# A selective-scan block on one core: the rows of each state's sum divided between ScalarE and VectorE block by block

## What is computed

```python
xz = hidden @ in_proj_w.T;  x, z = split(xz)          # 512 + 512 channels
u = silu(conv1d(x) + b)                               # causal, 4 taps
dt_low, B, C = split(u @ x_proj_w.T)                  # 16, 16, 16
delta = softplus(dt_low @ dt_proj_w.T + dt_b)
h = exp(delta * A) * h + delta * B * u                # per token, 512 channels x 16 states
y = sum over the 16 states of h * C  +  u * D
out = (y * silu(z)) @ out_proj_w.T
x1 = layernorm(hidden + out)                          # then router, experts, second layernorm
```

## Time and profile before

| | us |
|---|---|
| three runs | 4684.85, 4686.34, 4697.28 (median 4686.34) |
| the profiled execution, whole | 4683.41 |
| its span, first to last instruction | 4681.5 |
| eight chunks in the middle of stage 1 | 866.87 |
| busy in the whole span: PE, DVE, ACT, POOL | 3739.5, 3996.9, 3393.0, 3574.0 |

### The profile page before, as it was taken

The page is one execution under the profiler, slowest core; times in us unless marked ns, Lnnn a source line. Parts: engine busy times, 40 slices in busy tenths (PEclk is TensorE's granted clock), DMA queues, the critical chain, the costliest instruction groups (busy, mean ns, idle before and its releaser), DMA issues. The chain is left out here.

```text
span 4681.5 us, 57838 instructions
## 1 busy us (share of the span) xinstructions
PE 3739.5 (80%) x19154; PEld 2596.0 (55%) x19154; DVE 3996.9 (85%) x5099; ACT 3393.0 (72%) x5732; POOL 3574.0 (76%) x1744
## 2 busy tenths in 40 slices
PE   7888888888888888888888878888863199999990
PEld 3455555555555555555555555555553178888880
DVE  4999999999999999999999999999994667766645
ACT  5888787888888888878887888888861056555555
POOL 3888888888888888888888888888881156666643
PEclk8889898989888988988898998989875599999995
DMA  2454555554445545545554445545442123333328
GB/s 69 118 127 126 127 125 132 126 127 126 117 122 138 133 120 133 126 117 127 134 130 125 121 119 133 137 122 136 124 112 48 50 46 64 70 60 62 63 33 291
DMA packets 166374, 528.78 MB, mean 113 GB/s; under 512 B 31920, under 2 KB 97584, under 8 KB 118720
## 3 DMA queue, kind: packets, MB, share of 16 engines
q0 software_dynamic: 56832, 268.99, 29.5%
q1 hardware_dynamic: 104640, 239.32, 14.8%
q10 hardware_dynamic: 4608, 16.78, 0.9%
HBM read 221.47 MB, written 68.68 MB: 62 GB/s over the span
## 5 line engine op out<-in xcount | busy, mean ns | idle before, releaser
L369 POOL TENSOR_TENSOR dbu<-du,bb 128x2048 f32<-128x2048 f32 x512 | 2361.8, 4634 | 298.8 <-DVE h L736 274.0
L736 DVE TENSOR_TENSOR_SCAN h<-da,hlast,dbu 128x512 f32<-128x512 f32 x1536 | 1881.4, 1267 | 53.0 <-POOL dbu L369 41.9
L656 PE MATMUL ht<-ident,h 128*128 128x128 f32 x8192 | 1320.7, 308 | 594.6 <-DVE h L736 347.2
L419 ACT ACTIVATE da<-dl,negA 128x512 f32<-128x512 f32 x2048 | 1418.7, 698 | 468.9 <-DVE h L736 463.3
L656 PEld LDWEIGHTS ht<-ident,h 128*128 128x128 f32 x8192 | 1042.5, 157 | 1075.9 <-DVE h L736 555.2
L744 DVE SCALAR_TENSOR_TENSOR pair<-ht,ct,pair 128x512 f32<-128x512 f32 x896 | 639.0, 731 | 85.8 <-PE ht L656 85.4
L736 DVE TENSOR_TENSOR_SCAN h<-da,dbu 128x512 f32<-128x512 f32 x512 | 596.1, 1205 | 39.8 <-ACT da L419 25.0
L442 ACT ACTIVATE pair<-ht,ct 128x512 f32<-128x512 f32 x896 | 591.8, 687 | 50.7 <-PE ht L656 48.4
L589 PE MATMUL spare<-xin,win 128*128 128x512 f32 x1024 | 499.2, 617 | 40.3 <-DMA xin<-in_xt 26.0
L595 PE MATMUL spare<-xh,conv 128*128 128x512 f32 x1024 | 460.8, 592 | 2.2 <-ACT dl L456 1.5
L1149 POOL DMA_INDIRECT sums<-ot,idx x128 | 237.2, 1853 | 172.3 <-DVE ot L1425 130.7
(11 more groups left out here) (162 smaller groups left out, 5688.3 us busy)
## 6 DMA issues: line engine op xcount, KB each, us to landing
acc<-pair POOLq DMA_DIRECT2D x224, 1024.0 KB, 7.1
bb<-b_rows SPq DMA_DIRECT2D x128, 1024.0 KB, 5.2
xin<-in_xt SPq DMA_DIRECT2D x32, 512.0 KB, 4.4
xres<-in_x SPq DMA_DIRECT2D x32, 512.0 KB, 4.1
x_scores<-xres SPq DMA_DIRECT2D x32, 512.0 KB, 5.4
sums<-xres SPq DMA_DIRECT2D x32, 512.0 KB, 7.1
wraw<-in_w SPq DMA_DIRECT2D x16, 1024.0 KB
rows<-sums SPq DMA_DIRECT2D x32, 512.0 KB, 6.3
```

What stands on the lines that cost most here:

```text
L369: pool.tensor_tensor(dbu[n % 2][:], du[q][:], bb[part % 2][:, m:m + 1, :].to_broadcast([P, DT, CH]), ALU.mult).then_inc(dbu_done, 1)
L419: act.activation(da[DA_SLOT[m]][:], dl[q][:, dt, :], ACT.Exp, scale=negA[:, dt, n:n + 1]).then_inc(exp_done, 1)
L656: last = te.transpose(ht[HT_SLOT[m]][:, dt * P:(dt + 1) * P], h[n % 2][:, dt, b * P:(b + 1) * P], ident[:])
L736: dve.tensor_tensor_scan(h[n % 2][:, dt, :], da[DA_SLOT[n * DT + dt]][:], dbu[n % 2][:, dt, :], start, ALU.mult, ALU.add).then_inc(scan_do ...
```

## The change

The unit of division is no longer the state but the row block (n, b). Two new tables say which blocks ScalarE scales and VectorE adds, and in which slot: `SCALE_AT` has 36 blocks to a chunk (nine states' worth), `MAC_AT` 28 (seven). For each b by itself a block that is scaled starts a new sum and the added ones behind it belong to it, so each block row has nine sums (`TILE`), and a chunk has eight transfers that add, not seven. The sums have three homes besides `acc` of the chunk itself (`HOME`): `pair0`, `pair1` and the `acc` of the other parity, which is free between the turning of chunk c-1 and the start of chunk c+1. `add_sum` waits for both engines' last block of the sum, and the slots of the additions (`ADD_AT`) are new; slot 16 + n is slot n of the chunk behind. An adding block waits only for the scaled block that started its own row (`started_by`), where it used to wait for the same b of the state before.

The tables `STEPS`, `ACT_AT`, `DVE_AT` and `POOL_AT` are dealt anew, `BETWEEN` says how many of TensorE's steps in a slot come ahead of the fourth block's turning, and `xin` gets a second buffer, so that it is loaded a chunk earlier. No other instruction is added or removed.

```diff
-KIND = "ADADADADADADADAD"
-SUMS = KIND.count("A")
-ADD_AT = {t: min(LAST_OF[t] + 3, 17) for t in range(1, SUMS)}
+SCALE_AT = {(0, 0): [(14, 1)], (0, 2): [(15, 1), (15, 2)], (0, 3): [(15, 3)], (1, 2): [(0, 0), (0, 1)],
...
+MAC_AT = {(0, 1): [(15, 0)], (2, 1): [(1, 0), (1, 1)], (2, 2): [(1, 2)], (2, 3): [(1, 3)], (3, 3): [(2, 2)],
...
+ADD_AT = {1: 6, 2: 7, 3: 10, 4: 12, 5: 14, 6: 15, 7: 17, 8: 19}
+BETWEEN = [0, 1, 2, 2, 0, 1, 2, 0, 0, 0, 0, 2, 1, 2, 1, 1]
+TILE = {(n, b): sum((m, b) in ACT_ORDER for m in range(n + 1)) - 1 for n in range(16) for b in range(NB)}
+TILES = tile_of(15, 0) + 1
+HOME = [2, 0, 1, 3, 0, 1, 3, 0, 1, 0][:TILES]
+def started_by(n, b):
+
+    return next(k for k, (m, x) in enumerate(ACT_ORDER) if x == b and tile_of(m, x) == tile_of(n, b)) + 1
...
-        xin = a.sb("xin", [P, 2, CH])
+        xin = [a.sb(f"xin{i}", [P, 2, CH]) for i in range(2)]
...
+        def sum_tile(q, t):
+
+            return pair[HOME[t]] if HOME[t] < 2 else acc[q] if HOME[t] == 2 else acc[1 - q]
...
-                    pool.wait_ge(s, v)
-                    if not (is_first(c) and t == 1):
-                        pool.wait_ge(acc_in, 16 * (c * (SUMS - 1) + t - 1))
+                    pool.wait_ge(mac_done, c * N_DVE + macs_before_add(t))
+                    if scales_before_add(t):
+                        pool.sem_inc(pool_passed, 1)
+                        pool.wait_ge(scaled, c * N_ACT + scales_before_add(t))
+                    if not (is_first(c) and t == 1):
+                        pool.sem_inc(pool_passed, 1)
+                        pool.wait_ge(acc_in, 16 * (c * (TILES - 1) + t - 1))
...
-                    dve.wait_ge(scaled, c * N_ACT + scaled_by(n, b))
+                    dve.wait_ge(scaled, c * N_ACT + started_by(n, b))
```

More of the change, by code:

```diff
@@ new lines, with in_order @@
+MAC_AT = {(0, 1): [(15, 0)], (2, 1): [(1, 0), (1, 1)], (2, 2): [(1, 2)], (2, 3): [(1, 3)], (3, 3): [(2, 2)],
[4 rows of a table added]
+ADD_AT = {1: 6, 2: 7, 3: 10, 4: 12, 5: 14, 6: 15, 7: 17, 8: 19}
+BETWEEN = [0, 1, 2, 2, 0, 1, 2, 0, 0, 0, 0, 2, 1, 2, 1, 1]
+def in_order(table):
+    here = [(n, b) for slot in sorted(table) for n, b in table[slot] if n < slot[0]]
+    return here + [(n, b) for slot in sorted(table) for n, b in table[slot] if n >= slot[0]]
+ACT_ORDER, DVE_ORDER = in_order(SCALE_AT), in_order(MAC_AT)
+N_ACT, N_DVE = len(ACT_ORDER), len(DVE_ORDER)
@@ L89, in scaled_by, with tile_of @@
+TILE = {(n, b): sum((m, b) in ACT_ORDER for m in range(n + 1)) - 1 for n in range(16) for b in range(NB)}
+def tile_of(n, b):
+    return TILE[n, b]
+TILES = tile_of(15, 0) + 1
+HOME = [2, 0, 1, 3, 0, 1, 3, 0, 1, 0][:TILES]
+FIRST_OF = [next((n, b) for n, b in ACT_ORDER if tile_of(n, b) == t) for t in range(TILES)]
+ENDS = [(n, b) for n in range(16) for b in range(NB) if n == 15 or tile_of(n + 1, b) > tile_of(n, b)]
 def scaled_by(n, b):
-    return SUM_OF[n] * NB + b + 1
+    return ACT_ORDER.index((n, b)) + 1
@@ L94, in added_by, with scales_before_add, macs_before_add @@
 def added_by(n, b):
-    return KIND[:n].count("D") * NB + b + 1
+    return DVE_ORDER.index((n, b)) + 1
+def started_by(n, b):
+    return next(k for k, (m, x) in enumerate(ACT_ORDER) if x == b and tile_of(m, x) == tile_of(n, b)) + 1
+def scales_before_add(t):
+    return max([scaled_by(n, b) for n, b in ENDS if (n, b) in ACT_ORDER and tile_of(n, b) <= t], default=0)
+def macs_before_add(t):
+    return max([added_by(n, b) for n, b in ENDS if (n, b) in DVE_ORDER and tile_of(n, b) <= t], default=0)
@@ L186, in stage1 @@
         xin_in, xres_in, b_out, b_in = (
-            S("xin_in"), S("xres_in"), S("b_out"), [S(f"b_in{i}") for i in range(2)])
+            [S(f"xin_in{i}") for i in range(2)], S("xres_in"), S("b_out"), [S(f"b_in{i}") for i in range(2)])
         x1_out, x2_out = S("x1_out"), S("x2_out")
@@ L281, in _ @@
                 for c in range(2, n_chunks - 2):
-                    chunk(c, c % 2, (FR, P1, P2), True)
+                    chunk(c, c % 2, (FR, P1, P2), c < n_chunks - 3)
                 chunk(n_chunks - 2, 0, (FR, P1, P2), False)
@@ L432, in scale_by_c @@
                         act.wait_ge(s, v)
[L433 to L440, removed]
+                    if (n, b) == FIRST_OF[t]:
+                        s, v = home_free(c, t)
+                        if not is_first(c) or v > 0:
+                            act.wait_ge(s, v)
                     act.wait_ge(tr_done, (c * NS + n) * NB + b + 1)
-                    act.mul(target(q, n)[:, b, :], ht[HT_SLOT[n * NB + b]][:], ct[q][:, b, n:n + 1]).then_inc(scaled, 1)
+                    act.mul(target(q, n, b)[:, b, :], ht[HT_SLOT[n * NB + b]][:], ct[q][:, b, n:n + 1]).then_inc(scaled, 1)
                 def evacuate(kind, i, c, q):
@@ L541, in chunk @@
                                 save_last(c, n - 1)
[L542 to L548, removed]
+                            for m, b in SCALE_AT.get((n, k), ()):
+                                if m < n and scan:
+                                    scale_by_c(c, q, m, b)
+                                if m >= n and before:
+                                    scale_by_c(c - 1, 1 - q, m, b)
                             for what, i in ACT_AT.get((n, k), ()):
@@ L679, in chunk @@
                     for n in range(NS):
[L680 to L690, removed]
+                        if scan:
+                            turn(c, n, range(HT_RING))
+                        run(n, slice(0, BETWEEN[n]))
+                        if scan:
+                            turn(c, n, range(HT_RING, NB))
+                        run(n, slice(BETWEEN[n], None))
                 prev_of = {}
@@ L805, in chunk @@
                                 scan_tile(c, pos, n, k)
[L806 to L811, removed]
+                            for m, b in MAC_AT.get((n, k), ()):
+                                if m < n and live:
+                                    mac(c, q, m, b)
+                                if m >= n and before:
+                                    mac(c - 1, 1 - q, m, b)
                             for what, i in DVE_AT.get((n, k), ()):
```

63 lines of the change are left out of this document (35 added, 28 removed), and 23 rows, old and new, of tables (ACT_AT, MAC_AT, SCALE_AT, STEPS).

## The result

The changed kernel takes 4641.62 us, the median of four runs (4638.34 to 4655.15), against 4686.31 for the kernel before: a ratio of 0.9905, 95% interval 0.9884 to 0.9926. It is 45 us faster, where 174 were forecast. The time lies above the forecast range; the sign is right.

The account below looks back on a forecast made before the run. VectorE was taken to set the pace in stage 1: 4683.4 - 83 (blocks moved) - 93 (waits 2.9 instead of 5.8 us a chunk) + 3 = 4510, stated as 4512 us. Range 4447 to 4606, likeliest case 4475 to 4555.

Parts of the forecast that it names:

- The last addition: Issued behind product 3, it lands 7.1 us later, complete at 11.6; TensorE reaches Y at 11.8, so no wait.
- Rival 3: Last addition lands late at Y in slot 2; 4733 us at a 15 us landing; chance 0.07 with other slower ways.
- list of signs that it is wrong: New waits in the profile: Y on the adding transfer, scans on products, late exponentials; or stage 1's clock leaving 0.90.
- Blocks that move: VectorE does 28 blocks a chunk instead of 32, saving 83 us; ScalarE takes the four at no cost.
- GpSimd at the turn: At the turn of a chunk, the addition no longer delays product 2; VectorE's wait for products goes from 1.1 us to 0.
- Turned blocks: VectorE's wait for blocks turned by TensorE falls from 3.1 to 1.6 us a chunk, with XP still at 5.3 us.
- rival 2: Nearly all VectorE waits go, 0.9 us a chunk left, as shorter TensorE gaps end slow clock spells; 4449 us, chance 0.16.
- The exponentials: VectorE's wait for ScalarE's exponentials, late behind the two SiLU, stays 1.0 us a chunk, bounds 0.5 and 2.
- End of stage 1: The last two additions follow each other with nothing beside them, costing +3 us, bounds 0 and 8.

## Why the prediction was wrong

**The step that failed** is "The last addition": "then 7.1 to landing, so the sum is complete at 11.6. TensorE reaches Y at ... 11.8. No wait." Both times were right but for the landing. The 7.1 was the median of transfers none of which was started together with a load of B; moved to product 3, this one met the load and landed after 11.4. That is 4.3 us more, and 4.1 us of wait a chunk were measured, 131 us in 32 chunks; taking the clash away gave 140 to 153. The "about 1 us" that a late landing was to have free was not there either. It was reckoned from the fourth block of state 2, but VectorE waits earlier, at its own evacuation of Y. In the chunk whose addition starts at 1249.91 TensorE is through with C at 1257.13, 7.2 us later where 7.3 were forecast, and VectorE stands at that evacuation at 1258.15. The first turning of Y between the two takes 1.1 us, so nothing is left over, and VectorE waits 4.35 us. Rival 3 had the place and the mechanism, even the meeting with the load of B, and the prediction's list of signs that it is wrong begins with this very wait. It was given little because the slowest landing before was 9.2. But the rows of before could not show a clash that was not yet there: I walked the addition past GpSimd's queue and TensorE's, and did not look at what SyncE starts on the same event. The 3.4 us between 7.1 + 1 and 11.5 were not enough for slower than before, as the rival's own turning point of 14 us said.

**Blocks that move**: right. VectorE's own work fell from 102.5 to 100.0 us a chunk, forecast 99.9. ScalarE took its four blocks for almost nothing: it still waits 50.0 us in eight chunks for VectorE's scans, and VectorE's wait for its exponentials went from 8.4 to 9.9.

**GpSimd at the turn**: right in kind. The stall of 2.68 us for VectorE's last block is gone; the wait for products fell from 9.0 only to 6.4 us in eight chunks, not to 0. These eight chunks flatter the kernel before: from 1000 to 3000 us it waits 27.4 us for products and the changed kernel 9.1, so 1.5 us a chunk became 0.5.

**Turned blocks**: the mechanism was right and the size off to the good side. The term was 1.6 us a chunk; it measured (3.5 + 1.0 + 0.8) / 8 = 0.7, instead of 3.1. The shift of all blocks by one scan shows that the place behind the turning is needed for it. But the waits also go with the clock, the reason that rival 2 gives. In the eight chunks of the earlier trace rows XP takes 5.33 us in six, at a granted clock of 0.66 to 0.68, and 3.63 us in two, at 1.00. VectorE waits 3.6 to 4.6 us for turned blocks in each of the six and 0.55 and 0.56 in the two: 24.0 of the 25.1 us stand in the chunks with a slow XP. In the changed kernel XP takes 3.63 us at 1.00 in seven of the eight chunks and 4.35 at 0.83 in one. XP as a group in the same eight chunks, before and after:

```profile
L600 PE MATMUL spare<-u,wx 128*48 128x512 f32 x64 | 39.2, 773 | 0.0
...
L657 PE MATMUL spare<-u,wx 128*48 128x512 f32 x64 | 29.8, 609 | 0.0
```

The mean granted clock of 0.90 does not show this, because there are slow spells still, at another place: in the changed kernel it is 0.58 from 1384 to 1388 and 0.60 from 1490 to 1494, where TensorE turns blocks and does T ahead of XP, and XP behind them runs at 1.00. So the prediction was wrong to keep XP at 5.3 us. A fast XP alone is not enough, though. With the blocks one scan earlier its matmuls take 596 ns on average, and turned blocks are waited for 93.0 us. How much of the 2.4 us a chunk came from the fast XP and how much from the slack stays open.

The Trainium skill, "TensorE: Matmul & The Clock Gate", "What's actually happening", says that the clock is at 1.2 GHz when TensorE has been idle and at 2.4 GHz once it has been kept busy. The trace agrees in the changed kernel: the stretch at 0.58 from 1384 stands right behind 3.06 us of idle time, and the XP at 1387.97, with TensorE busy in between, is at 1.00. Nor is TensorE busier as a whole, 83.1% of the eight chunks before and 82.5% after, with a mean of 0.90 both times. But the idle time just before does not settle the level: in the kernel before the XP at 1089.02 and the one at 1195.75 both start 0.6 us behind 2.37 us of idle time, and the first is at 1.00, the second at 0.67.

**The exponentials** were 1.2 us a chunk for 1.0. **End of stage 1**: 32 x (108.36 - 107.01) = 43 us less from the chunks, 40.2 less in the span, so +3 us for the two ends of stage 1 together, as taken.

With the clash gone the sum comes out, 4489 and 4502 us measured for the two times that this kernel was timed, 4512 forecast, but partly by luck. From 1000 to 3000 us VectorE waits 41.7 us there, 2.1 a chunk for the forecast 2.9: turned blocks are 1.3 below their term, products 0.5 and exponentials 0.2 above theirs, and Y 0.2 below. The range was wrong because its upper end took all waits at their old size, and no new one.

## What to carry to other kernels

When a transfer is moved, list what every other queue starts on the same event. A median time to landing holds only for what the transfer met in the trace from which it was taken; two of 1 MB together took 11.4 us here where one took 7. And where a slot table is tuned to within a scan of the engine that it waits for, the distance between producer and consumer counts as much as the work that is moved: all of VectorE's blocks one scan (1.19 us) earlier cost 188 to 201 us here, where four blocks a chunk less on VectorE were worth 83. And a mean granted clock that stays the same does not say that the slow spells stay where they were.

## What the runs showed of the hardware

Two transfers of 1 MB that start together, one adding into SBUF from GpSimd's queue and one a broadcast load from SyncE's, moved 217 to 246 GB/s together while the DMA engines were full (0.98 to 1.10), where the addition alone moved 193 to 201 (0.96 and 0.98). So they shared the engines rather than the second filling gaps of the first: the addition's landing went from 6.9 to 7.6 us to 11.4 to 11.5. Started 2.8 us behind it, the load added only about 1 us (7.9 to 8.5).

The same XP, eight matmuls, took 3.63 us at a granted clock of 1.00 and 5.33 us at 0.66 to 0.68.
